# One wait less in front of GpSimd's subtraction in the gated stage

## What is computed

```python
h = jnp.einsum('bchw,oc->bohw', x, w_in)
h = jax.lax.conv_general_dilated(h, w_dw, window_strides=(1, 1), padding='SAME', feature_group_count=2 * HID, ...)
x1, x2 = jnp.split(h, 2, axis=1)
h = jax.nn.gelu(x1, approximate=False) * x2
y = jnp.einsum('bchw,oc->bohw', h, w_out)
...
f = jnp.fft.rfft2(yp.astype(jnp.float32)) * fft_w
yp = jnp.fft.irfft2(f, s=(P, P))
```

## Time and profile before

| | us |
|---|---|
| median of 3 runs | 11,620.83 (11,619.16 to 11,628.11) |
| profiled execution | 11,619.18 |
| its span | 11,617.4 |
| TensorE busy | 10,347.6 (89%) |
| VectorE busy | 7,587.5 (65%) |
| GpSimd busy | 5,467.0 (47%) |
| ScalarE busy | 3,289.6 (28%) |
| L941 in the gated stage | 595.5 (128 of 4,652 ns) |

### The profile page before, as it was taken

How to read it: one execution, slowest core, us unless ns; L and a number is a source line. 1 busy time by engine, 2 the same in 40 slices (tenths; PEclk the granted TensorE clock), 3 DMA queues, 4 the chain that set the end, 5 groups by cost and what they waited for, 6 DMA issues and landing times. The chain is left out here.

```text
span 11617.4 us, 229342 instructions
## 1 busy us (share of the span) xinstructions
PE 10347.6 (89%) x76604; PEld 9514.8 (82%) x76604; DVE 7587.5 (65%) x19436; ACT 3289.6 (28%) x3654; POOL 5467.0 (47%) x5025
## 2 busy tenths in 40 slices
PE   0899999788879998999979998999959899898989
PEld 0899999555569998998879998988859899898964
DVE  6444444322248886878878886876658788787864
ACT  0222222222222353014422451045543233222210
POOL 0666666233335554555545554554434444444410
PEclk9999999899999999999989999997779999999999
DMA  9888888799976567769956567789967777777779
GB/s 177 143 145 147 143 148 145 141 195 193 191 157 176 139 179 161 181 152 213 199 142 177 138 181 162 177 172 217 206 132 124 120 120 126 118 122 117 124 214 364
DMA packets 1987203, 1910.07 MB, mean 164 GB/s; under 512 B 1236650, under 2 KB 1876496, under 8 KB 1914256
## 3 DMA queue, kind: packets, MB, share of 16 engines
q1 hardware_dynamic: 1986448, 1900.86, 79.1%
HBM read 781.57 MB, written 578.81 MB: 117 GB/s over the span
## 5 line engine op out<-in xcount | busy, mean ns | idle before, releaser
L741 POOL TENSOR_TENSOR rl_wide<-rl_wide,rl_state 96x512 f32<-96x512 f32 x510 | 818.2, 1604 | 779.4 <-ACT rl_state L655 779.4
L273 PE MATMUL du_sum<-du_high,sw_down_high 96*96 96x256 f32 x6132 | 1081.7, 285 | 61.1 <-DVE du_high L335 33.6
L273 PE MATMUL du_sum<-du_low,sw_down_high 96*96 96x256 f32 x6132 | 1115.6, 290 | 0.1
L273 PE MATMUL du_sum<-du_high,sw_down_low 96*96 96x256 f32 x6132 | 1074.8, 284 | 0.0
L1471 PE MATMUL gf_four<-gf_full_high,l_w_hid_full_high 128*128 128x256 f32 x3072 | 895.3, 291 | 110.1 <-DMA gf_left<-gf_full_high 109.8
L1471 PE MATMUL gf_four<-gf_full_low,l_w_hid_full_high 128*128 128x256 f32 x3072 | 884.0, 288 | 81.9 <-DMA gf_left<-gf_full_low 81.9
L935 POOL TENSOR_TENSOR gf_sums<-gf_block 96x520 f32<-96x520 f32 x512 | 602.3, 1205 | 688.2 <-DVE gf_hid_a L1555 681.6
L941 POOL TENSOR_TENSOR gf_full_low<-gf_sums,gf_full_high 96x2080 fp32r<-96x2080 f32 x128 | 595.5, 4652 | 634.1 <-DVE gf_hid_a L1555 629.1
L273 PEld LDWEIGHTS du_sum<-du_high,sw_down_high 96*96 96x96 f32 x6132 | 828.2, 164 | 69.0 <-DVE du_high L335 35.4
L1471 PE MATMUL gf_four<-gf_full_high,l_w_hid_full_low 128*128 128x256 f32 x3072 | 882.1, 287 | 0.0
L1471 PE MATMUL gf_four<-gf_left,l_w_hid_left_twice 128*128 128x256 f32 x3072 | 881.2, 287 | 0.0
(11 more groups left out here) (219 smaller groups left out, 29990.3 us busy)
## 6 DMA issues: line engine op xcount, KB each, us to landing
du_wide<-x SPq DMA_DIRECT2D x32, 3072.0 KB, 17.0
up<-du_wide SPq DMA_DIRECT2D x32, 3072.0 KB, 20.9
rl_wide<-up SPq DMA_DIRECT2D x128, 768.0 KB, 16.1
rl_wide<-x SPq DMA_DIRECT2D x128, 768.0 KB, 16.7
x<-rl_wide SPq DMA_DIRECT2D x128, 768.0 KB, 13.4
down<-du_lines SPq DMA_DIRECT2D x28, 3072.0 KB, 23.7
du_lines<-down SPq DMA_DIRECT2D x28, 3072.0 KB, 16.4
right<-rl_lines SPq DMA_DIRECT2D x28, 3072.0 KB, 23.6
```

What stands on the lines that cost most here:

```text
L273: mm = self.nc.tensor.matmul(self.half_line(r, c), w[0:kk, k, :], x[0:kk, (r - 1) % RING, 2 * c:2 * c + 2, k:k + PAIRS], start=(n == 0 and ...
L741: nc.gpsimd.tensor_tensor(at, at, by_sub_block(row), ALU.add).then_inc(placed, 1)
```

## The change

The subtraction in `pool_batch` loses its hold on `quiet`. The hold on `rounded`, which stands ahead of it, stays, and so does the one on `quiet` in front of the sums. The two other users of `pool_batch` pass no `quiet` and are as before.

```diff
             self.ph.hold(pool, self.rounded, AHEAD + NSTRIP * b + u + 1)
-            if quiet is not None:
-                self.ph.hold(pool, quiet, 2 * (NSTRIP * b + u) + 2)
             g.tensor_tensor(self.full["low"][u % SLOTS][0:C2, :, :], rows,
                             self.full["high"][u % SLOTS][0:C2, :, :], ALU.subtract).then_inc(self.rest, 1)
```

## The result

| | before | changed |
|---|---|---|
| median, us | 11,624.5 (4 runs, 11,619.2 to 11,629.3) | 12,011.7 (4 runs, 12,003.1 to 12,020.1) |
| profiled execution, us | 11,619.2 | 12,007.0 |
| its span, us | 11,617.4 | 12,005.0 |

A forecast was written before the change was run, and what follows sets the result against it. TensorE was taken as the bound, VectorE close behind; holding VectorE 4.65 us makes it the bound at 22.17 us a strip. +392, taken as +396 for first strips, on 11,619.2 gives 12,015 us, range 11,940 to 12,095.

The forecast's parts named there:

- The bound and the slack: Gated stage: TensorE bounds at 18.02 us a strip; VectorE needs 17.52, so it has 0.50 us of slack.
- the sum: Gated stage, first to last gated subtraction: 122 distances of 22.17 us plus three batch changes, 2860.4 against 2468.3, +392 us.
- Where the subtraction goes: GpSimd's subtraction starts 0.18 us after the rounding, 1.7 us earlier than before, inside VectorE's first product.
- The price: VectorE's products held by GpSimd's subtraction: between 0 and 4.65 us lost per strip.
- The upper end: Whole subtraction lost to VectorE, 4.65 us per strip, giving 22.17 us a strip; full hold, chance 0.80.
- The changes of batch: Three distances between subtractions that hold a chain of stores and loads: stay at 51.9 us each.
- 0 to 19 us: First strips of the four batches: whether they are held too was open, 0 to 4 x 4.65 us more.
- What it hides: TensorE's waits for low parts and its clock loss, about 1.5 us, fall where TensorE would wait for VectorE.
- slower by more: Rival: TensorE's clock stays at 1.2 GHz long enough each strip to bound again; 24.0 us a strip, 12,245 us; chance 0.03.
- faster: Rival: engines don't hold each other; earlier low parts shorten waits, 41 to 60 us gained, about 11,570 us; chance 0.04.
- The direction that no row showed: A VectorE product arriving while GpSimd's long subtraction runs: taken as blocked for the whole of it, by the skill's rule.

The follow-up runs named there:

- shorter pause: Kernel before, both gates kept, plus a 3900-column VectorE fill ahead of the third product of each strip's second half: 11,985 us, ratio 1.0299.
- two pieces: Changed kernel with the subtraction cut into two instructions of 1040 columns: 12,029 us, ratio 1.0333 to the kernel before.
- both edits: Changed kernel (second gate gone) with SyncE's store also issued one strip later: 12,028 us, ratio 1.0337 to the kernel before.
- without gates: Changed kernel with the hold on `quiet` in front of the sums removed as well: 12,241 us, ratio 1.0521 to the kernel before.
- longer pause: Kernel before, both gates kept, plus a 5200-column VectorE fill ahead of the third product of each strip's second half: 12,235 us, ratio 1.0511.
- the fills: Changed kernel with the subtraction replaced by two GpSimd fills that read nothing, about 4.6 us together: 11,554 us, ratio 0.9924 to the kernel before.

## Why the prediction was right

*The bound and the slack.* VectorE's 17.52 us a strip, read from two rows at the stage's start, carried the sum. The table bears it out: 17.52 plus the held time (or the pause) gives the strip within 0.1 us in six kernels, over 0.9 to 4.4 us. In the four others it is 0.3 to 0.9 us short, for which see below. And where the same time is lost on VectorE with nothing held (shorter pause), the kernel is as slow, within 0.3%.

*Where the subtraction goes.* It starts 0.18 us behind the rounding, as worked out. It was to meet the first product and meets the second: with VectorE as the bound, the products start 0.32 us before the rounding ends, and not 0.04. I took the relation of the two from strips that TensorE paces. It changes nothing, since the loss is the same in either gap.

*The price.* The upper end, the whole subtraction, was the right choice: first come, first served, for whole instructions. Its size was 4.65 and measured 4.36: from the held product's start (9810.80) the subtraction takes 4.49 us more, and the product ends 0.29 us behind it, where its own length is 0.42 (4.49 + 0.29 - 0.42 = 4.36). So some 0.15 us of work overlap at either end. That is 0.29 x 122 = 35 us too much in the sum.

*The changes of batch.* They were to stay at 51.9 us and are 56.8 to 57.1, 15 us more in all. The held product lies inside that distance, since the subtraction now starts ahead of the hold. The first strips of the four batches, which I had left open, are not alike: in two nothing is held and the distance behind is 16.7 us in place of 22.17, in two the fourth product is held for its full 4.4 us and the distance is 21.2 (16.7 + 4.4 = 21.1). That is 13 us less than in the sum, so that the "0 to 19 us" for these strips are made up by the 15 of the batch changes and nothing is left of them. The 118 other distances are 21.91 us on average, 30.6 us less in all. Together that is 28.5 us less: 2831.9 us where the sum has 2860.4, and +363.6 in place of +392.

*What made up for it.* The spans differ by 387.6 us. 363.6 of it lies between the first and the last of these subtractions. The first one comes 16.7 us later (8687.53 against 8670.82), nearly all of it time of the stages before, which the change doesn't touch; 7.3 us lie behind the last. So that 12,015 and 12,012 agree to 3 us is in part luck: the sum was 28 us too high, and 24 us came from outside the stretch that it describes.

*What it hides.* TensorE's clock isn't hidden whole, as I had it. In some 20 of the changed kernel's strips the distance is 22.1 to 22.6 us in place of 21.85. Most of these lie between 9000 and 9360 us, where VectorE waits some 0.3 us at a time for TensorE and the granted clock is 0.92 on average; over 9440 to 9800 us it is 0.95 and nearly all distances are 21.8 or 21.9. In the kernels with two pieces and with both edits most strips are of this kind. Without the stage's start and the batch changes, VectorE's waits for TensorE are 10 us in the changed kernel, 31 with both edits, 39 with two pieces, 46 without gates and 81 with the longer pause: per strip 0.08, 0.26, 0.32, 0.38 and 0.66. The sum falls short by 0, 0.26, 0.34, 0.26 and 0.94 us, so these waits are about what it lacks. The clock over 9500 to 10,000 us, a stretch without a change of batch, falls in the same order: 0.95, 0.93, 0.92, 0.90 and 0.88. So the two kernels that lose most per strip (12,241 and 12,235 us) come near the rival "slower by more", in which TensorE's clock decides. Which strips get it, and why, no run shows. As predicted, the waits for low parts nearly vanish (4 are left), and the run with both edits shows that their removal is worth nothing in the changed kernel, while it is worth 1.0% in the kernel before.

*The rival "faster".* Its condition was false, but its price can be read from the fills: 80 us, where I had 41 to 60. An earlier low part is worth more than the waits it shortens (36 us). What the rest is no run shows; TensorE's slower time behind each wait is a guess.

*The direction that no row showed.* A product that comes while the subtraction runs takes 4.78 us instead of 0.42 in the changed kernel, and beside GpSimd's fills, which only write, it keeps its 0.42. The Trainium skill (SBUF — State Buffer, "Who interferes with whom") says both: that the one that comes later is blocked while the other runs, and that a GpSimd instruction that only writes doesn't contend with two SBUF inputs on VectorE. These two runs agree.

## What to carry to other kernels

Where VectorE's instructions with two SBUF inputs and GpSimd's reading instructions can fall together, the one that comes later stands still until the other is through (4.4 us for a subtraction of 4.9); so a long GpSimd instruction wants a moment at which no such product is due. Cutting it helps only when there are more pieces than products left: each product waits for one piece, so two pieces cost 4.2 us where two products were left, four 2.0 and eight 0.9. Price a wait by what stands on the other side of it: this one cost GpSimd 629 us of idle time that nobody needed and saved 387. VectorE, with 17.52 us of work in a strip of 18.02, became the bound as soon as something stopped it for longer than the 0.5 us between.

## What was new about the hardware

- In this trace a VectorE product that a GpSimd instruction holds is recorded as a long instruction (4.78 us), not as idle time; a rise in busy time with an unchanged count is the sign to look for.
- GpSimd's copy with one SBUF input holds a product until it is through (products of 2.05 us against copies of 2.16 and 2.11); its fills of 1.83 and 2.81 us don't.
- VectorE's instructions with one SBUF and one PSUM input keep their 0.42 us beside GpSimd's sums, which hold products for 0.8 to 1.0 us each when the two meet.
- GpSimd gives the turn away between two of its instructions even if the next is ready: products of 1.43 us against four pieces of the subtraction, 0.88 against eight.
- A fill on VectorE between two products had 1.03 us of idle time ahead of it at 5200 columns and 0.76 at 3900. The cause is open.
